# Moving a small constant product, two loads and a weight split out of the start-up order of a fused attention and FFN kernel

## The reference

```python
# step 1: x = x + attn(cond(x))
h   = gelu(gelu(cond_128 @ W0 + b0) @ W1 + b1)
att = softmax(h @ W2 + b2)                       # 64 batches x 8 experts
mixed = einsum('boi,bih->boh', einsum('bk,koi->boi', att, weight), x) + att @ bias_k
q, k, v = mixed @ Wq, mixed @ Wk, mixed @ Wv     # 32 heads, one k and one v
o = softmax(q * k / sqrt(32)) @ v                # 32 x 32 scores per row
x = x + broadcast(o)
# step 2: x = x + ffn(conv(x))
u = conv1d(x, weight, groups=4, taps=9) + (cond_128 @ c_weight.T)[:, :, None] + fside[:, None]
x = x + u @ (scale * (unpack4(packed) - zero)).T + bias
```

## Time and profile before

| | us |
|---|---|
| median of 3 executions | 430.84 |
| lowest, highest | 427.61, 431.04 |
| profiled execution, its own time | 430.84 |
| profiled execution, its span | 428.8 |
| TensorE busy | 412.5 (96%) |
| VectorE busy | 365.4 (85%) |
| GpSimd busy | 341.0 (80%) |
| ScalarE busy | 226.9 (53%) |

### The profile page before, as it was taken

How to read it: one execution, slowest core, us unless ns; L and a number is a source line. 1 busy time by engine, 2 the same in 40 slices (tenths; PEclk the granted TensorE clock), 3 DMA queues, 4 the chain that set the end, 5 groups by cost and what they waited for, 6 DMA issues and landing times.

```text
span 428.8 us, 6661 instructions
## 1 busy us (share of the span) xinstructions
PE 412.5 (96%) x2195; PEld 348.2 (81%) x2195; DVE 365.4 (85%) x603; ACT 226.9 (53%) x465; POOL 341.0 (80%) x317
## 2 busy tenths in 40 slices
PE   5987799899999999999999999999999999999997
PEld 4987688778888888888888888888888888888885
DVE  2897999999989899899989799999989899983421
ACT  4853665565455273747456364637364465562700
POOL 4042939679677999999999979899979989999920
PEclk9998999999999999999999999999999999999999
DMA  8988256370737375655736290918074371816112
GB/s 322 411 322 339 99 171 235 130 258 4 221 110 280 136 227 197 212 210 157 268 98 226 77 338 27 336 74 293 29 244 179 77 249 39 285 45 230 49 52 98
DMA packets 21608, 78.82 MB, mean 184 GB/s; under 512 B 5688, under 2 KB 5816, under 8 KB 17208
## 3 DMA queue, kind: packets, MB, share of 16 engines
q1 hardware_dynamic: 21272, 76.98, 51.2%
q10 hardware_dynamic: 288, 1.18, 0.8%
HBM read 60.88 MB, written 17.27 MB: 182 GB/s over the span
## 4 chain that ended last, share of the span: by engine, by line
PE 82%; DVE 6%; issue 1%; ACT 0%; DVEq 0%
PE p_f L1158 53%; PE p_conv L1152 19%; PE p_sm L1128 8%; PE p_sm L1137 1%; DVE den L836 1%; DVE c_lo L881 1%; DVE xc L875 1%; DVE prob L827 1%; DVE prob L832 1%; DVE p_sm L844 1%; DVE p_ut L892 0%; DVE prob L840 0%; DVE xc L867 0%; ACT u_sb L616 0%; DVE rden L848 0%
## 5 line engine op out<-in xcount | busy, mean ns | idle before, releaser
L1158 PE MATMUL p_f<-w_ffn,u_hi 128*128 128x512 f32 x512 | 195.7, 392 | 0.0
L1158 PE MATMUL p_f<-w_ffn,u_lo 128*128 128x512 f32 x512 | 194.8, 390 | 0.0
L616 ACT ACTIVATE u_sb<-p_conv,u_bias,cols_sb 128x128 f32<-128x128 f32 x256 | 94.8, 459 | 40.9 <-PE p_conv L1152 38.8
L1158 PEld LDWEIGHTS p_f<-w_ffn,u_lo 128*128 128x128 f32 x512 | 96.2, 188 | 20.5
L1158 PEld LDWEIGHTS p_f<-w_ffn,u_hi 128*128 128x128 f32 x512 | 96.2, 188 | 20.5
L452 POOL TENSOR_TENSOR c_lo<-xc,c_hi 128x516 fp32r<-128x516 f32 (+1 forms) x66 | 82.6, 1262 | 11.9 <-ACT c_hi L606 7.6
L463 POOL TENSOR_TENSOR xn<-xn,bias_n 128x1024 f32<-128x1024 f32 x32 | 76.3, 2403 | 5.4 <-DMA xn<-xn_in_in 5.4
L606 ACT ACTIVATE c_hi<-xc 128x516 fp32r<-128x516 f32 (+1 forms) x68 | 41.2, 609 | 67.5 <-POOL xc L444 61.3
L439 POOL TENSOR_TENSOR xc<-xc,o_c 128x384 f32<-128x384 f32 x60 | 54.3, 905 | 24.5 <-DMA o_c<-o_dram 23.2
L905 DVE TENSOR_TENSOR xn<-p_f,xn 128x512 f32<-128x512 f32 x64 | 43.4, 679 | 23.8 <-PE p_f L1158 23.4
L892 DVE STREAM_TRANSPOSE p_ut<-u_sb 128x512 f32<-128x512 f32 (+1 forms) x68 | 45.8, 680 | 15.8 <-ACT u_sb L616 15.7
(11 more groups left out here) (114 smaller groups left out, 461.4 us busy)
## 6 DMA issues: line engine op xcount, KB each, us to landing
xc<-xc_in_in SPq DMA_DIRECT2D x16, 1032.0 KB, 9.1
xn<-xn_in_in SPq DMA_DIRECT2D x16, 1024.0 KB, 6.9
out<-xn SPq DMA_DIRECT2D x31, 512.0 KB, 7.4
xt<-xt_in_in SPq DMA_DIRECT2D x15, 1024.0 KB, 5.8
o_c<-o_dram SPq DMA_DIRECT2D x15, 256.0 KB
xn<-wq_in SPq DMA_DIRECT2D x4, 512.0 KB, 12.1
xt<-wq_in SPq DMA_DIRECT2D x1, 1024.0 KB, 6.3
xn<-wq_in SPq DMA_DIRECT2D x1, 1024.0 KB, 8.3
```

The lines of the kernel that those rows point to most:

```text
L616: ins = eng.activation(u_sb[:, g % 2, i * P:(i + 1) * P], p_conv[g % 2][:, i * P:(i + 1) * P], ACT.Identity, bias=u_bias[:, g, bat:bat + 1 ...
L1158: return mm(p_f[half][:, :], u[:, (k // TU) % 2, r, t * P:(t + 1) * P], w_ffn[:, r, 512 * half:512 * half + 512], **flags)
```

## The change

The context product leaves the start. Its weights are no longer a part of `cols_sb`, widened on the chip by GpSimd; they come already widened by a transfer of their own, called ctx (`load_context`, 128 rows of 512 floats, 256 KB). `context()` stands between two halves of `project(1, 1, ...)` and writes into `p_ut[0]`; ScalarE's `bias_of_u`, four activations that read it, stands behind `z_copy(1)`; `copy_o(0, 0)` waits for it. VectorE's small product `cbs` moves a little later. SyncE's list has x2 ahead of cw, then ctx, c0 and c1, then n0, and x3 behind n0. On TensorE, `mix(1)` stands one half earlier, the first three `copy_o` stand ahead of `project(3, 0, 0)`, `keep_busy` has other places and counts, and `conv(0, 0)` stands ahead of `project(3, 1, ...)`. On ScalarE one `convert_weights` stands ahead of `exp(0, 1)`, and `z_copy(2)` behind `c_high(0, 0)`.

```diff
-... ("brow", W3), ("ctxw", G * CG)):
+... ("brow", W3)):
...
+            def load_context():
+                eng.dma_start(ctx_sb[:, :, :], ctx_w).then_inc(s_ctx, 16)
+
...
             eng.wait_ge(s_w3, 2)
             load_x(1)
+            load_x(2)
             load_conv_weights()
-            load_x(2)
+            load_context()
             load_c(0)
-            load_x(3)
+            load_c(1)
             eng.wait_ge(s_w3, 4)
             load_n(0)
-            load_c(1)
+            load_x(3)
             load_bias()
...
-            eng.wait_ge(s_small, 16)
-            eng.tensor_copy(ctx_sb.rearrange("p g (r c) -> p g r c", r=R),
-                            ctxw_sb.rearrange("p (g c) -> p g c", g=G).unsqueeze(2).broadcast_to([P, G, R, CG])).then_inc(s_ctx, 1)
...
             convert_weights(0, 1)
             exp(0, 0)
             z_copy(1)
+            bias_of_u()
+            convert_weights(1, 0)
             exp(0, 1)
+            c_high(0, 0)
             z_copy(2)
-            convert_weights(1, 0)
-            c_high(0, 0)
             exp(1, 0)
...
             def context():
-                eng.wait_ge(s_ctx, 1)
+                eng.wait_ge(s_ctx, 16)
                 for g in range(G):
-                    last = mm(p_conv[1][:, B * g:B * g + B], ctx_sb[:, g, :], cond_sb, start=True, stop=True)
+                    last = mm(p_ut[0][:, B * g:B * g + B], ctx_sb[:, g, :], cond_sb, start=True, stop=True)
                 last.then_inc(s_cb, 1)
...
                     if p == 0:
                         eng.wait_ge(s_sel, 1)
+                        eng.wait_ge(s_ub, G)
...
-            context()
...
-            eng.wait_ge(s_ub, G)
...
             project(1, 1, 0)
+            context()
             project(1, 1, 1)
             project(2, 0, 0)
             project(2, 0, 1)
+            mix(1)
             project(2, 1, 0)
-            mix(1)
             project(2, 1, 1)
-            keep_busy(p_conv[0], 2)
-            project(3, 0, 0)
             copy_o(0, 0)
             copy_o(0, 1)
             copy_o(0, 2)
+            keep_busy(p_conv[0], 5)
+            project(3, 0, 0)
+            copy_o(0, 3)
             project(3, 0, 1)
+            conv(0, 0)
             project(3, 1, 0)
-            copy_o(0, 3)
             project(3, 1, 1)
-            conv(0, 0)
-            keep_busy(p_conv[1], 3)
             copy_o(1, 0)
```

More of the change, by code:

```diff
@@ L40, with block_program @@
 NCOLS = 0
-for _name, _n in (("cond", B), ("w0", P), ("w1", P), ("w2", KE), ("b0", 1), ("b1", 1), ("cbias", G), ("scale", 1), ("zero", 1), ("own", 4), ("b2", KE), ("mixb", P), ("brow", W3), ("ctxw", G * CG)):
+for _name, _n in (("cond", B), ("w0", P), ("w1", P), ("w2", KE), ("b0", 1), ("b1", 1), ("cbias", G), ("scale", 1), ("zero", 1), ("own", 4), ("b2", KE), ("mixb", P), ("brow", W3)):
     AT[_name] = slice(NCOLS, NCOLS + _n)
     NCOLS += _n
-def block_program(nc, xt_in, xc_in, cols, mix_w, wq, wvk, conv_w, packed_t, xn_in, bias_in, out):
+def block_program(nc, xt_in, xc_in, cols, mix_w, wq, wvk, conv_w, ctx_w, packed_t, xn_in, bias_in, out):
     ctx = ExitStack()
@@ L100, in block_program @@
         cols_sb = sb("cols_sb", [P, NCOLS])
-        cond_sb, w0_sb, w1_sb, w2_sb, b0_sb, b1_sb, cbias_sb, sc, zero, own, b2_all, mixb_all, brow_all, ctxw_sb = (
+        cond_sb, w0_sb, w1_sb, w2_sb, b0_sb, b1_sb, cbias_sb, sc, zero, own, b2_all, mixb_all, brow_all = (
             cols_sb[:, at] for at in AT.values())
@@ L555, in _ @@
             eng.activation(att[:, 1, :], att[:, 0, :], ACT.Exp, scale=-1.0, bias=att_s[:, 0:1], accum_out=att_s[:, 1:2]).then_inc(s_act0, 1)
[L556 to L562, removed]
             eng.wait_ge(s_wvk, 16)
@@ L625, in u_high, with bias_of_u @@
                 eng.activation(ut_view(u_hi, p, g), columns(p_ut[g % 2], p).rearrange("p (n r c) -> p n r c", n=len(batches(p)), r=R), ACT.Copy).then_inc(s_uh, 1)
+            def bias_of_u():
+                eng.wait_ge(s_cb, 1)
+                eng.wait_ge(s_cbs, 1)
+                for g in range(G):
+                    eng.activation(u_bias[:, g, :], p_ut[0][:, B * g:B * g + B], ACT.Identity, bias=cbs[:, g:g + 1], scale=sc).then_inc(s_ub, 1)
             def load_x6():
@@ L743, in _ @@
             eng.wait_ge(s_small, 16)
-            eng.tensor_scalar(cbs[:, :], cbias_sb, sc, None, ALU.mult).then_inc(s_cbs, 1)
             eng.wait_ge(s_pe0, 3)
@@ L771, in _ @@
             eng.tensor_scalar(zp[:, 1:2], zero, ZLIM, -ZLIM, ALU.min, ALU.max).then_inc(s_zp, 1)
+            eng.tensor_scalar(cbs[:, :], cbias_sb, sc, None, ALU.mult).then_inc(s_cbs, 1)
             eng.wait_ge(s_zp, 1)
@@ L1444 @@
              "scale": rows(arr("L0_ffn_scale")), "zero": rows(arr("L0_ffn_zero_point")), "own": own, "b2": rows(arr("L0_cond_b2")),
-             "mixb": mixb, "brow": brow, "ctxw": arr("L0_cond2_c_weight").T}
+             "mixb": mixb, "brow": brow}
+    ctx_w = arr("L0_cond2_c_weight").T.reshape(P, G, 1, CG)
     arrays = {
@@ L1452 @@
         "conv_w": conv_w.reshape(P, 2, G, P),
+        "ctx_w": np.broadcast_to(ctx_w, (P, G, R, CG)).reshape(P, G, P),
         "packed_t": arr("L0_ffn_packed_weight").T.reshape(4, 32, 4, 2, HALF).transpose(2, 1, 0, 3, 4).reshape(P, R, HALF),
```

## The result

The changed kernel takes 431.89 us in the median of 13 executions (431.26 to 432.94), the kernel before 428.97 on the same chip (427.51 to 431.43, also 13). The ratio is 1.0069, with a 95% interval of 1.0048 to 1.0091: 2.9 us slower, inside the 1% that was called no change. Forecast were 429.5 us, 1.3 less than the kernel before; the sign is wrong. The profiled execution of the changed kernel took 432.14 us with a span of 430.2.

The account below looks back on a forecast made before the run. TensorE, busy 412.5 of 428.8 us, was taken as the bound, its steady work starting when VectorE finishes near 80 us. Terms -1.8 + 0.4 + 0.1 = -1.3 us on 430.84 gave 429.5 us, range 426.8 to 432.4.

Parts of the forecast that it names:

- the second rival: TensorE's clock halves in the new wait for the context's weights, delaying work by 1.7 us; 431.4 to 432.4 us; chance 0.22.
- A clock that is down at 30 us: Sign on TensorE that the prediction is wrong; it expected the granted clock at 1.00 through 35 us.
- Before the wait TensorE has worked 3 us without a gap: Argument given against TensorE's clock falling in the 2.7 us wait for the context's transfer.
- by the bounds of this case alone: The main case's own range for the kernel time, 428.7 to 430.8 us; the main case's chance was 0.48.
- the term of -1.8: On VectorE, add_first(0, 0) starts at 36.2 instead of 37.96 because the first copy_o comes earlier: -1.8 us.
- x3's 2.2 us: In the earlier trace x3 landed 4.7 us behind c0, 2.2 more than its size costs.
- an interlock of 0.4 us: Loss where TensorE's path and VectorE's gain meet four times at additions and copies: +0.4 us, bounds 0 and 1.1.
- a third rival: x3 landing after 41.3 delays project(4) and eats the gain; called no change, 430.9 us; chance 0.15.
- the context's landing: The context's weights, transferred behind x2 and cw, land at about 29.4 us, between 28.3 and 31.6.
- the order in which the transfers landed: Transfers of SyncE's queue land in order of issue, so the context's weights cannot pass x2 and cw.
- nothing from the start: No gain from the context's matmuls leaving the start; the extra tiny VectorE instruction costs +0.1 us, between 0 and +0.2.
- the steady part: From 52 to 80 us and beyond, the front's -1.3 us is carried on unshortened, with no other waits after 80.

Follow-up runs that it names:

- e2: Changed kernel with the context's transfer issued behind the packed weights, before x1, so the context doesn't wait: 432.27 us, ratio 1.0066 to the kernel before.
- e5: Kernel before with 20 instead of 4 filling matmuls in TensorE's wait for x3: 428.65 us, ratio 0.9988.
- e4: Changed kernel with SyncE's old list of loads, the context's transfer right behind cw: 428.41 us, ratio 0.9998 to the kernel before.
- e1: Changed kernel with 18 filling matmuls in the context's wait: 431.19 us, ratio 1.0044 to the kernel before.
- e7: Changed kernel with 18 filling matmuls before the context and 24 instead of 10 before unit 3: 429.50 us, ratio 1.0013 to the kernel before.
- e3: Kernel before with the change's new orders on SyncE, TensorE and ScalarE, the context still at the start: 432.16 us, ratio 1.0063.
- e10: Kernel before with x3 alone moved behind c1 and n0 in SyncE's list: 433.21 us, ratio 1.0104.
- e9: e2 with x3 alone moved forward in SyncE's list, to behind c0: 429.61 us, ratio 1.0009 to the kernel before.
- e12: Kernel before with only the context moved (transfer behind cw, product between unit 1's halves, bias_of_u behind z_copy(1)), other orders kept: 429.11 us, ratio 1.0006.
- e8: e4 with 12 filling matmuls ahead of the first copy_o: 428.70 us, ratio 0.9999 to the kernel before.
- e11: e5 with GpSimd's split of the conv weights moved behind its subtract(0, 1): 428.57 us, ratio 1.0001 to the kernel before.
- e14: e5 with 8 filling matmuls added ahead of mix(0): 429.5 us, ratio 1.0005 to the kernel before.

## Why the prediction was wrong

**What failed first is the size of the clock's fall.** It was the second rival, with 0.22: "TensorE's clock falls in the context's wait". The mechanism came as told, but it was sized by the 3.4 us of the earlier trace rows, at a cost of 1.7. It lasted 6.8 us (28.4 to 35.2), of which TensorE worked 6.1: 3.1 us of loss where 1.7 were reckoned, and it decided at a landing of 29.0 where the rival needed 29.5 and more. With that size the rival's own sum, at a landing of 29.0 instead of 29.4, is -1.3 - 0.4 + 3.1 - 0.4 = +1.0; the two chains differ by 1.1 us at 80 us, the two profiled executions by 1.3 (430.84 and 432.14). A clock that is down at 30 us was one of the signs that the prediction had named of its being wrong. "Before the wait TensorE has worked 3 us without a gap" was no argument against it: in e2, where TensorE had worked from 23.1 to 35.9 with one gap of 0.76, the clock fell too, in a longer wait. Nor does the range that is given "by the bounds of this case alone", up to 430.8, hold its own bounds: a landing at 31.6 puts the first addition 2.2 us later, +0.4 in place of -1.8, and that is 431.2 or more.

**What failed second is the term of -1.8, and with it the base.** It closes VectorE's 2.13 us of the earlier trace rows, and those belong to an execution in which x3 took 7.2 us to land and the clock fell behind the wait for it. e5, with the same lists but for the filling, has x3 land after 4.7 us and no hole, and e4, all of the change but the loads, takes what the kernel before takes. Against its own base the sum was nearly right: with the clock kept from the context on, `project(4)` begins at 50.38 (e1) and 50.49 (e7) where 50.2 was forecast, and e7's median is 429.50, the 429.5 of the forecast. But the kernel before begins `project(4)` at 49.25 when x3 lands early (e5), not at 51.60, and takes 428.3 at the full clock, so what was booked as a gain of 1.3 us is a loss of 1.2. The two other executions that were known, 427.61 and 431.04, could have said that 430.84 lies at the upper end of a spread, and the earlier trace rows that its clock had fallen just ahead of the hole. The prediction read both, called x3's 2.2 us "odd" besides, and took the hole for the kernel's.

**What failed third is x3's price.** Its landing was forecast at 39.4 and was 39.0. Its cost was taken as part of an interlock of 0.4 us, with a third rival only for a landing after 41.3. With the rest of the new list it costs about 1 us at the full clock: `project(4)` begins at 50.49 in e7 and at 49.73 in e4, and the medians at the full clock are 429.61 and 428.31. And it makes a wait of 1.4 to 3.7 us. Of e1, e2, e3 and e10, all with x3 at 38.6 to 39.9 and no more filling there than the changed kernel's, not one execution is at the full clock. In the profiled ones of e2 and e3 the clock falls as that wait ends, in e10's 1.6 us behind it, and in e1's, after 1.41 us, not at all.

**The sum.** 431.89 less 428.97 is 2.9. Keeping the clock gives back 2.4 (e7); the old list of loads gives back the whole (e4), since the falls hang on it too, and of that x3's place alone is 2.7 (e9 against e2). The two overlap, so they don't add up to 2.9. Which of the two waits, the context's or x3's, brings the clock down in an unprofiled execution differs from one to the next; removing the context's alone gained 0.7 (e1) or nothing (e2).

**Right** were: the context's landing (29.0 for 29.4) and wait (2.25 for 2.7), the order in which the transfers landed (x2 27.1, cw 28.4, the context's 29.0; this agrees with the Trainium skill, DMA: Bandwidth & Descriptors, section Queues, rings and completion order, that was weighed there), `subtract(0, 0)` at 1.22, nothing from the start (e12: a ratio of 1.0006), and the steady part, which carried the front's 1.1 us unchanged.

**Still open** is where the remaining falls of the kernel before begin. Some were seen at 23 to 24, at the idling ahead of `mix(0)` (e1 and e9 to e12), and one at 35; what makes x3 land 2.5 us later in one execution than in another is open too; in unprofiled executions only their sum is known. Whether the new order of TensorE is worth some tenths at the full clock is open too: e9's three executions say 0.8, e4's five and e8's nine say nothing.

## What to carry to other kernels

Before a hole in a profile is booked as a gain, look at the granted clock ahead of it and at the spread of the times: one execution at 0.995 can show a hole that others don't have. Look also at the landing times of the loads around it, and at the same load in a second profile. A wait of 2 to 4 us of TensorE can cost more than its length, 3.1 us more in the changed kernel and 3.4 in e2. Filling matmuls laid into it ahead of the instruction that waits cost nothing that these runs can tell, as long as they end before the wait does; where they started only as the wait ended (ahead of `mix(0)`), they cost their own length. When a load is put back in a queue, price every engine that waits for it in the new order, and not only the engine that the change is about.

## What the runs showed of the hardware

TensorE's clock fell 1.6 us into a wait of 2.25 us in the changed kernel, only as a wait of 3.67 us ended in e2, and 1.6 us behind the end of one of 3.42 us in e10. It stayed at half for 6.8 us in the first two and for 3.4 in the third, though TensorE worked on. Idling of 1.2 us ahead of `mix(0)` had a fall in it or up to 1.1 us behind it in the profiled executions of e1 and e9 to e12, and none in those of e2 and e4, whose TensorE has the same instructions up to there as that of e1, e9 and e12. The same wait of TensorE can thus cost nothing in one execution and microseconds in the next, and a program's times lie apart by it: 428.3 us at the full clock and 430.8 at 0.992 and lower here.

The same 1 MiB load, from the same place of the same list, landed 4.7 (e5), 4.8 (e11), 6.3 (e14) and 7.2 us (the kernel before) after its issue. One profile shows only one of these.

The Trainium skill (TensorE: Matmul & The Clock Gate, Part 1 on the clock gate) says that the chip's look at TensorE's activity runs on by itself and isn't restarted by a kernel, so that the same kernel can differ from run to run. That fits the groups above; no run here varied it by itself, so it is not shown as their cause.
